# Half-sums by accumulating transfers, and the convolution's taps on TensorE, in a fused state-space and FFN kernel

## What is computed

```python
x = x + mamba(layernorm(x))
x = x + (layernorm(x) @ W.T + bias)          # W = scales * (codes - 128)

# mamba:
x, z = split(h @ in_proj_w)
xc = silu(conv_b + sum_k conv_w[:, k] * x shifted by 3 - k)      # 4 taps
dt_r, B, C = rmsnorm of the three parts of xc @ x_proj_w
dt = softplus(dt_r @ dt_proj_w + dt_bias)
h[t] = exp(dt[t] * A) * h[t-1] + dt[t] * B[t] * xc[t]            # 16 states a channel
ys[t] = sum over the 16 states of h[t] * C[t]
y = (ys + D * xc) * silu(z)
out = y @ out_proj_w.T
```

## Time and profile before

| | |
|---|---|
| time, median of 3 runs | 4657.14 us (4652.04 to 4660.07) |
| the profiled execution's own time | 4652.27 us, of which the span of the trace is 4650.4 us |
| busy: TensorE, VectorE, GpSimd, ScalarE | 95%, 90%, 87%, 76% of the span |
| mean granted TensorE clock | 0.98 of full speed |
| a middle step (six of the eight of a chunk) | 33.20 us |
| last step of a chunk, first step of the next | 36.89 us, 39.09 us |
| a chunk, so | 275.2 us |

### The profile page before, as it was taken

How to read it: one execution, slowest core, us unless ns; L and a number is a source line. 1 busy time by engine, 2 the same in 40 slices (tenths; PEclk the granted TensorE clock), 3 DMA queues, 4 the chain that set the end, 5 groups by cost and what they waited for, 6 DMA issues and landing times.

```text
span 4650.4 us, 80289 instructions
## 1 busy us (share of the span) xinstructions
PE 4425.4 (95%) x26656; PEld 4020.1 (86%) x26656; DVE 4164.3 (90%) x5745; ACT 3537.7 (76%) x8848; POOL 4034.5 (87%) x2942
## 2 busy tenths in 40 slices
PE   7788999999999999999999999999999999998879
PEld 6577889989898998989899898998989899897769
DVE  3899999999999999999999899999999999999871
ACT  3787787877878787787878878787887878777650
POOL 0898989989899998989899899999989999899870
PEclk9889999999999999999999999999999999999889
DMA  7324344353544435353444535335353443533232
GB/s 252 135 82 160 104 156 147 121 184 129 184 137 159 147 129 179 137 181 128 150 156 137 186 122 184 128 131 191 120 184 129 175 144 115 184 129 135 96 106 84
DMA packets 160286, 678.57 MB, mean 146 GB/s; under 512 B 21120, under 2 KB 30080, under 8 KB 110720
## 3 DMA queue, kind: packets, MB, share of 16 engines
q1 hardware_dynamic: 141440, 639.88, 39.6%
q10 hardware_dynamic: 18432, 33.56, 1.9%
HBM read 618.32 MB, written 55.05 MB: 145 GB/s over the span
## 4 chain that ended last, share of the span: by engine, by line
PE 65%; DVE 14%; POOL 8%; issue 7%; DMA 3%; ACT 2%; SPq 1%; POOLq 0%; DVEq 0%; ACTq 0%
PE gx L594 15%; PE ys L574 13%; PE g L767 12%; PE ys L614 12%; DVE hb L1378 9%; PE g L689 6%; POOL dbx L486 5%; DVE hc L1326 3%; POOL half L494 2%; PE ys L604 2%; PE ys L624 2%; PE hb L875 1%; DVE gx L1270 1%; DMA b_scratch<-ssmT 1%; DMA ybuf<-in_wf_scales 1%
## 5 line engine op out<-in xcount | busy, mean ns | idle before, releaser
L1378 DVE TENSOR_TENSOR_SCAN hb<-hb,dbx 128x512 f32<-128x512 f32 x2048 | 2496.7, 1219 | 110.8 <-ACT hb L1083 77.2
L486 POOL TENSOR_TENSOR dbx<-dtx,bb 128x1024 f32<-128x1024 f32 x1024 | 2421.2, 2364 | 68.9 <-DVE hb L1378 43.9
L1083 ACT ACTIVATE hb<-dt,a_neg 128x256 f32<-128x256 f32 x4096 | 1789.3, 468 | 66.3
L494 POOL TENSOR_TENSOR half<-hc 128x512 f32<-128x512 f32 x1024 | 1305.3, 1275 | 86.0 <-DVE hc L1326 85.1
L1326 DVE TENSOR_TENSOR hc<-hb,cb 128x512 f32<-128x512 f32 x2048 | 1376.2, 672 | 0.0
L574 PE MATMUL ys<-half,ident 128*128 128x256 f32 x4096 | 1057.2, 390 | 115.4 <-POOL half L494 99.1
L574 PEld LDWEIGHTS ys<-half,ident 128*128 128x128 f32 x4096 | 764.1, 194 | 242.9 <-POOL half L494 131.4
L767 PEld LDWEIGHTS g<-wo,ybuf 128*128 128x128 f32 x7680 | 909.3, 194 | 27.5 <-issue 15.2
L614 PE MATMUL ys<-xnT,wz 128*128 128x256 f32 x4096 | 931.5, 381 | 1.3 <-DVE ybuf L1337 1.3
L594 PE MATMUL gx<-xnT,wx 128*128 128x256 f32 x3968 | 903.6, 382 | 21.8 <-issue 11.0
L767 PE MATMUL g<-wo,ybuf 128*128 128x128 f32 x7680 | 915.0, 277 | 9.0 <-issue 9.0
(11 more groups left out here) (105 smaller groups left out, 2739.1 us busy)
## 6 DMA issues: line engine op xcount, KB each, us to landing
wz<-in_win SPq DMA_DIRECT2D x128, 1024.0 KB, 4.8
wx<-in_win SPq DMA_DIRECT2D x124, 1024.0 KB, 4.8
wo<-in_wout SPq DMA_DIRECT2D x123, 1024.0 KB, 5.0
wf<-wf_scratch SPq DMA_DIRECT2D x113, 512.0 KB, 3.9
xc_scratch<-xcn ACTq DMA_DIRECT2D x128, 256.0 KB, 3.7
xcs<-xc_scratch SPq DMA_DIRECT2D x128, 256.0 KB, 5.0
bb<-bc_scratch SPq DMA_DIRECT2D x64, 512.0 KB, 8.8
cb<-bc_scratch SPq DMA_DIRECT2D x64, 512.0 KB, 8.0
```

The costliest lines, as they stand in the source:

```text
L486: nc.gpsimd.tensor_tensor(dbx[:, k % 2, :].rearrange("p (n t) -> p n t", n=NQ), dtx[:, S % 2, a, :].unsqueeze(1).to_broadcast([P, NQ, T]), ...
L494: nc.gpsimd.tensor_tensor(half[:, k % 4, :], hc[:, k % 2, 0:HALF], hc[:, k % 2, HALF:GW], ALU.add).then_inc(halves, 1)
L1083: ins = nc.scalar.activation(h[:, m * T:(m + 1) * T], dt[:, j % 2, a, :], ACT.Exp, scale=a_neg[:, ds((2 * j + a) * N + 2 * v + m, 1)])
L1378: nc.vector.tensor_tensor_scan(h[:], h[:], dbx[:, k % 2, w * UW:(w + 1) * UW], 0.0, ALU.mult, ALU.add).then_inc(scans, 1)
```

## The change

**Sums.** In each half the products of groups 0 and 1 now go to a tile of their own, `hd`, with one buffer for each of the two groups (`hc` serves groups 2 and 3). When both are there, a DMA issued by GpSimd adds group 1 onto group 0 in SBUF (`add_group_pair`, `accum_op`), and one GpSimd add (`pair_sum`) makes one `half` of the result. So a half has three sums in place of four, a step has six, and `half` has three buffers. TensorE adds two parts of the first two sums of each half and only one of the third; VectorE adds the other part to PSUM (`last_sum`) ahead of `y_gate`. TensorE thus has 5 matmuls with the identity a half, not 8.

**Taps.** Once, at the start, GpSimd makes diagonal matrices of the convolution's weights, which are stored to DRAM (`wt_scratch`). In each step SP loads six of 128 x 128 (`wt`, 384 KB), and TensorE adds the three taps of two tiles onto `gx` by six matmuls (`pair_taps`). VectorE's six instructions go away for all pairs but the first nine.

**Bias.** One DMA a chunk, issued by GpSimd in the chunk's first step, adds the bias from DRAM to the rows (1 MB). The four GpSimd instructions and the tile `biasb` go away.

```diff
+SUMS = 6
+FIRST_TWO = (1, 3)
+HS = 3
+        wt = sb("wt", [P, 2, KC - 1, P])
+        hd = sb("hd", [P, 2, GW])
-        half = sb("half", [P, 4, HALF])
+        half = sb("half", [P, HS, HALF])
...
+                    if nx.x_job(nx_last):
+                        load_taps(S + PAIRS + 2)
                     if nx.next_scan(nx_last):
                         sp.wait_ge(z_mm, after(S + 2))
...
+            def sum_place(S, i):
+                n = SUMS * S + i
+                pool.wait_ge(sum_mm, after(n - HS + 1))
+                if n >= HS and (n - HS) % 3 == 2:
+                    pool.wait_ge(y_ready, after((n - HS) // 3 + 1))
+                return half[:, n % HS, :]
+            def add_group_pair(S, a):
+                pool.wait_ge(hcs, after(UNITS * S + UNITS // 2 * a + 4))
+                pool.dma_start(hd[:, 0, :], hd[:, 1, :], accum_op=ALU.add).then_inc(hd_acc, 16)
+            def pair_sum(S, a):
+                pool.wait_ge(hd_acc, 16 * (2 * S + a + 1))
+                nc.gpsimd.tensor_tensor(sum_place(S, FIRST_TWO[a]), hd[:, 0, 0:HALF], hd[:, 0, HALF:GW],
                                         ALU.add).then_inc(halves, 1)
...
-                    for k in range(1, 8):
-                        if k == 7 and zz:
-                            inflow_of(S + 1)
-                        group_of_b(S, k, c)
-                        if k >= 2:
-                            group_sum(S, k - 2)
-                        elif not (first and c == 0):
-                            group_sum(S - 1, 7)
-                        if k == 5 and j % 2 == 0 and st.ffn:
-                            add_bias(c - 2, j // 2)
+                    products(1)
+                    if not (first and c == 0):
+                        group_sum(S - 1, 1, 3)
+                    products(2)
+                    add_group_pair(S, 0)
+                    products(3)
+                    products(4)
+                    group_sum(S, 0, 2)
+                    pair_sum(S, 0)
+                    products(5)
+                    group_sum(S, 0, 3)
+                    if first and st.ffn:
+                        add_bias(c - 2)
+                    products(6)
+                    add_group_pair(S, 1)
+                    if zz:
+                        inflow_of(S + 1)
+                    products(7)
+                    pair_sum(S, 1)
                     if zz:
                         carry_of(S + 1)
                         group_of_b(S + 1, 0, (S + 1) // PAIRS)
-                    group_sum(S, 6)
+                    group_sum(S, 1, 2)
...
+            def pair_taps(q):
+                pe.wait_ge(tap0, after(q + 1))
+                pe.wait_ge(wt_in, landed(q - PAIRS))
+                for a in range(2):
+                    for tap in range(KC - 1):
+                        mm = nc.tensor.matmul(gx[:, a * T:(a + 1) * T], wt[:, a, tap, :], xpre[:, a, tap:tap + T],
+                                              start=False, stop=(tap == KC - 2), skip_group_check=True)
...
-                        group(0)
                         x_in_proj(0)
-                        group(1)
                         ss_transpose()
                         x_in_proj(1)
+                        group(0)
+                        group(1)
+                        dt_proj()
                         group(2)
-                        group(3)
-                        dt_proj()
                         out_proj(2)
+                        x_taps()
                         out_proj(3)
                     z_in_proj(1)
-                    group(4)
+                    group(3)
+                    if edge:
+                        x_taps()
                     z_in_proj(0)
-                    group(5)
...
+            def last_sum(SP, a):
+                n = SUMS * SP + 3 * a + 2
+                dve.wait_ge(sum_mm, after(n + 1))
+                dve.wait_ge(halves, after(n + 1))
+                nc.vector.tensor_tensor(ys[a][:, 0:T], ys[a][:, 0:T], half[:, n % HS, T:HALF], ALU.add
+                                        ).then_inc(summed, 1)
```

164 lines of the change are left out of this document (99 added, 65 removed).

## The result

The changed kernel takes 5362.22 us (median of 4 runs, 5359.44 to 5373.77), the kernel before 4655.44 us on the same chip (4652.04 to 4660.07). The ratio is 1.1522, with a 95% interval from 1.1502 to 1.1542: the change costs 707 us. The forecast was 5230 in a range from 4970 to 5650.

The account below looks back on a forecast made before the run. TensorE was taken as the bound (33.2 us a middle step); GpSimd's transfers make it 38.0. A chunk costs 8 x 4.8 - 2.4 = 36.0 us more, 16 chunks 576, on 4652.3: 5230 us, range 4970 to 5650.

Parts of the forecast that it names:

- The mechanism: GpSimd, in order, waits for VectorE's products before issuing each step's two transfers, so later work comes late; +4.8 us a middle step.
- I: Time that issuing one transfer holds GpSimd: taken as 1.0 us, between 0.33 and 1.27.
- path A: First half: late group 3 `dbx`, GpSimd's last sum, then TensorE's 14.4 us; step of 35.7 + I, 36.7 us.
- B: Second half: transfer issued after unit 11's product, its landing, `pair_sum`, TensorE's 4.3 us; step of 31.5 + I + D, 38.0.
- C: Second half with short D: GpSimd's own `dtx` and `dbx` behind the issue, sum, TensorE; step of 35.2 + 2I, 37.2.
- D: Time from the start of a 512 KB accumulating transfer's issue to its landing: taken as 5.5 us, from 3.9 to 8.
- middle step: One of a chunk's six steps between its edges, `ffn` to `ffn`: claimed 38.0 us against 33.2, +4.8.
- edge steps: A chunk's first and last steps: 2.4 of their 4.1 us of TensorE waits were to coincide with new ones.
- TensorE's floor: TensorE's work in a middle step: sums -2.6 us, taps +2.6 us, so it stays at 33.2 us.
- The clock: Rival, chance 0.13: TensorE's clock falls behind its waits; its forecast size is not in the text given.
- Slow landing: Rival: transfers land in D = 8 us, adding 998 us, 5650 us and more beyond; chance 0.13, half beyond 5650.

Follow-up runs that it names:

- the run without the transfer: Changed kernel without the two hd<-hd transfers a step (group 1 of each half left out), GpSimd's waits for VectorE's products kept: 5062.89 us, ratio 1.0886.
- the taps-back run: Changed kernel with the convolution's taps moved from TensorE back to VectorE, behind unit 11's product: 5748.66 us, ratio 1.2359.

## Why the prediction was right, and where it was off

- **The mechanism held.** GpSimd's first transfer waits for unit 3's product, 4.54 us; group 3's `dbx` comes late, and VectorE stands still 1.64 us ahead of unit 6's scan (forecast: 0.6 + I, 1.6). Unit 3's product ends at t = 10.08 (forecast: 10.1). TensorE waits 1.43 and 1.53 us for the first half's sums. The three paths lie within 0.6 us of each other, by their formulas (with I = 0.9, path A is 36.6, B 37.2, C 37.0) as in the trace.
- **Two signs did not come.** GpSimd was to stand idle about 1 us ahead of `half<-hd` in the second half and does so for 0.20, since D is shorter than I took and its own work behind the issue longer. TensorE's busy time was to stay near 4425 us at full clock and is 4591.5: a middle step shows 34.23 us for 33.20 at a clock of 1.00 (rows behind a wait are longer, the first sums 2.26 us for 1.89), and the edge steps 37.66 and 39.34 for 35.71 and 36.20, at 0.96 and 0.93.
- **The middle step**, 37.8 us for 38.0, is right by two errors that nearly cancel. D is 4.84 and not 5.5 (an estimate; no trace shows that both operands count for the landing, and the changed kernel's queue counts 512 KB for each transfer), I 0.9 and not 1.0 (the queue holds GpSimd 0.60 us, and the `dbx` behind it takes 2.68 for 2.37). Against that each transfer starts 0.3 us behind the end of the product and not 0.1, twice, and the sum and TensorE's work behind it take 0.2 more than I had.
- **TensorE's floor** of 33.2 was right: -2.6 for the sums, +2.6 for the taps, which alone give 35.79. That the taps, `wt` and VectorE's gain are worth nothing by themselves was right too, except that the taps also keep `wo`'s load out of the transfer's way, which no term had.
- **The edge steps failed by size.** I had taken 2.4 of their 4.1 us of waits as cover, so +7.2 us for the two. They grew by 14.45. The last step grows by 5.8 where its 1.2 us of waits should have covered some. Its waits did not cover the new ones but grew by 3.85 us, to 5.04, and TensorE's busy time by 1.96. The step of 42.70 us, on TensorE:

```profile
2615.13 1.13 PE L689 MATMUL ys<-xprojw,xcn 128*128 128x96 f32 x8 [2.35 <-DVE ybuf L1446]
...
2641.34 1.79 PE L645 MATMUL ys<-half,ident 128*128 128x256 f32 x4 [1.96 <-POOL half L551]
2642.93 3.80 PE L680 MATMUL gx<-xpre,wt 128*128 128x256 f32 x12
```

`pair_proj` waits 2.35 us for the later `y_gate` (0.47 before), the second half's sum comes 1.96 us late, and the sum and the taps behind it run at a slow clock (0.68 over the 5.4 us from 2641.30; 3.80 us for the twelve instructions, 2.76 in a middle step). Four of the twelve last steps are at full clock throughout and take 40.9 to 41.9 us, so the clock is about 1.6 of the 5.8 us. In the first step the bias transfer, which I had priced at its issue, 16 us in all, delays the landing behind it and costs 5.8 us a chunk, 85 us in all. The prediction weighed that transfer against GpSimd's time and not against the landing of the transfer issued behind it.
- **The start and the end.** The twelve whole chunks behind the first `ffn` take 3825.5 us for 3302.6, 318.8 a chunk for 275.2: 43.6 more each, 523 in all. The steps of the usual lengths would make 42 of it; the rest are the longer middle steps. The first `ffn` comes 79 us later (783.37 for 704.09), near the 87 of two such chunks. The rest, 106 us, lies behind the twelve in two chunks and the end, 19 more than two such chunks cost. The last chunk's first seven steps, the kernel before and then the changed one:

```profile
4240.43:4484.45 244.02, 204.95 (x1165) 179.39 (x1164) 207.07 (x256) 173.75 (x425) 222.16 (x162) 0.89 0.29 101
```

```profile
4882.71:5185.99 303.28, 198.32 (x1082) 172.58 (x1080) 211.01 (x268) 172.14 (x420) 213.07 (x159) 0.82 0.38 104
```

TensorE has less work there, and its clock falls from 0.89 to 0.82 as the waits grow; a step costs 8.5 us more, not 4.6.
- **The clock**, a fall of it behind TensorE's waits, to which the prediction gives 0.13, came in part. The case for it is the kernel before, in its last chunk: 0.74 over 12 us in which TensorE waits for sums. In the changed kernel, in 61 of the 72 middle steps the clock stays at 1.00; in the other 11, in 8 of the 12 last steps and in 11 of the 12 first ones it is 0.90 to 0.96, and lower still in the last chunk. In the run without the transfer such a fall, to 0.58 over 4.1 us, costs 1.64 us.
- **Slow landing**, D = 8, did not come in the middle steps of the changed kernel (4.8), but it was only 2.25 us away, as the taps-back run shows. The place of one load decides between the two, and no term of the sum looked at it.

In sum, of the 132 us between 5230 and the measured time, twelve chunks have 12 x 7.6 = 91: 6.9 of the 7.6 are the edge steps (14.1 us on average for 7.2), 0.6 the middle ones (6 x 4.9 for 6 x 4.8). The start has 7, and the last two chunks and the end have 34. That the total lies within 3% rests on the mechanism for the middle steps; for the edges the forecast was too low by half.

What stays open: why the clock falls behind a wait of 1.53 us in one step and stays behind one of 1.54 in another (I did not test it), and what makes the 2.8 us by which a chunk's first step is longer even without the bias's transfer (41.93 for 39.09).

## What to carry to other kernels

On an engine that takes its instructions in order, as GpSimd does here (the wait ahead of the transfer moved group 3's `dbx` from t = 7.6 to 11.0), price a new transfer first by the wait that it puts ahead of the next instruction, then by its landing on the longest chain, and only last by the work that it saves: here 3 us a step came off GpSimd and the step grew by 4.6. Look at what every other queue issues within some us of a transfer that someone waits for: a 1 MB load 0.34 us ahead of it cost 519 us here, and an edit that only took work off the busiest engine had put it there. When the bound is one engine's work, move the smallest piece that the next engine can take: one addition of 0.34 us a step on VectorE brought 36 us, where the three parts of the change together cost 707.
